# A fused decoder on one core: paired matmuls, GpSimd's share of the projections, and ScalarE's exponentials that write their own sums

## What is computed

```python
x = _layernorm(x + _L0_attn_ref(x, ...))         # self-attention, 16 heads of 16, quaternion projections, q and k normed
x = _layernorm(x + _L0_xattn_ref(ctx, x, ...))   # two memory hops over 77 context rows
x = _layernorm(x + _L0_ffn_ref(x, ...))          # 8 experts, 256 -> 1024 -> 256, gelu
x = _layernorm(x + _L1_attn_ref(x, ...))         # causal exponential convolution, gelu, projection
x = _layernorm(x + _L1_xattn_ref(x, ctx, ctx, ...))  # cross-attention, 16 heads of 16, 77 keys
x = _layernorm(x + _L1_ffn_ref(x, ...))          # gated layer, 256 -> 768 -> 256, everything quantised
```

```python
attn = jnp.einsum('bhqd,bhkd->bhqk', q, k) / jnp.sqrt(jnp.float32(Dh))
attn = jax.nn.softmax(attn, axis=-1)
out = jnp.einsum('bhqk,bhkd->bhqd', attn, v)
...
def act_qdq(x):
    qmax = 2.0 ** (ACT_BITS - 1) - 1.0
    scale = jnp.maximum(jnp.max(jnp.abs(x)) / qmax, 1e-12)
    return jnp.clip(jnp.round(x / scale), -qmax - 1.0, qmax) * scale
```

## Time and profile before

| | |
|---|---|
| median of 3 runs | 869.48 us |
| the profiled execution | 869.56 us, its span 867.8 us |
| busy: TensorE, weight loads | 752.1 us (87%), 431.9 us (50%) |
| busy: VectorE | 522.2 us (60%) |
| busy: ScalarE | 552.0 us (64%) |
| busy: GpSimd | 191.5 us (22%) |
| mean granted TensorE clock | 0.958 |
| chain that ended last | TensorE 38%, ScalarE 30%, VectorE 21%, issue 7% |

### The profile page before, as it was taken

One profiled execution on the slowest core, in us unless ns is written; L12 is line 12 of the kernel. 1 busy time (PEld: TensorE's weight loads), 2 busy tenths in 40 slices (PEclk: granted clock), 3 DMA queues, 4 the chain that ended last, 5 costly groups with the idle time before them and its releaser, 6 DMA issues.

```text
span 867.8 us, 10805 instructions
## 1 busy us (share of the span) xinstructions
PE 752.1 (87%) x3849; PEld 431.9 (50%) x3849; DVE 522.2 (60%) x1088; ACT 552.0 (64%) x941; POOL 191.5 (22%) x214
## 2 busy tenths in 40 slices
PE   4986899999999988998799998679899979994397
PEld 2642111111111137977688886445656844441286
DVE  4899332322111129779524648869967567898886
ACT  3656999999999962324132152575777433598991
POOL 1778000000000003215003202385543200000013
PEclk9996999999999999999899999799999989998599
DMA  7210213131364410302055000002100000000002
GB/s 198 100 25 1 49 33 78 26 85 25 87 202 66 118 47 1 97 1 98 1 194 193 1 1 1 0 0 74 37 0 2 1 1 0 1 0 0 0 25 73
DMA packets 57373, 42.13 MB, mean 49 GB/s; under 512 B 36866, under 2 KB 54120, under 8 KB 57192
## 3 DMA queue, kind: packets, MB, share of 16 engines
q1 hardware_dynamic: 57176, 41.31, 17.2%
q10 hardware_dynamic: 144, 0.13, 0.1%
HBM read 28.59 MB, written 4.46 MB: 38 GB/s over the span
## 4 chain that ended last, share of the span: by engine, by line
PE 38%; ACT 30%; DVE 21%; issue 7%; DMA 1%; SPq 1%; POOL 1%; DVEq 0%; POOLq 0%; ACTq 0%
ACT arena L535 24%; PE banks L1786 5%; PE banks L1778 5%; PE banks L1579 5%; PE banks L1567 5%; PE banks L1679 3%; PE banks L1651 2%; DVE arena L894 2%; DVE arena L902 2%; DVE arena L1186 2%; PE banks L1476 2%; DVE arena L790 2%; ACT arena L712 1%; ACT arena L698 1%; PE banks L1599 1%
## 5 line engine op out<-in xcount | busy, mean ns | idle before, releaser
L535 ACT ACTIVATE arena<-banks 128x1024 f32<-128x1024 f32 x256 | 235.4, 1094 | 3.1 <-PE banks L1349 3.0
L1349 PE MATMUL banks<-arena 128*32 128x512 f32 x1024 | 138.1, 611 | 2.2 <-ACT arena L535 0.8
L855 DVE COPY arena<-banks 128x512 f32<-128x512 f32 x16 | 11.1, 692 | 180.6 <-PE banks L1349 180.6
L1335 PE MATMUL banks<-arena 64*128 64x512 f16 x512 | 99.4, 390 | 23.1 <-ACT arena L535 9.4
L359 POOL TENSOR_SCALAR arena<-arena 128x2 f32<-128x2 f32 (+1 forms) x38 | 12.7, 334 | 462.2 <-DVE arena L897 462.2
L1335 PEld LDWEIGHTS banks<-arena 64*128 64x128 f16 x512 | 24.7, 93 | 166.8 <-ACT arena L535 154.4
L1778 PE MATMUL banks<-arena 128*128 128x512 f32 x192 | 85.9, 609 | 3.9 <-DVE arena L1197 3.7
L626 ACT ACTIVATE arena<-banks,arena 128x77 f32<-128x77 f32 x256 | 58.9, 363 | 22.2 <-DVE arena L1110 22.1
L1786 PE MATMUL banks<-arena 128*128 128x256 f32 x192 | 44.5, 397 | 26.6 <-ACT arena L733 26.6
L1579 PE MATMUL banks<-arena 128*128 128x256 f32 x256 | 58.2, 389 | 5.8 <-DVEq L1032 5.8
L1778 PEld LDWEIGHTS banks<-arena 128*128 128x128 f32 x192 | 37.3, 196 | 51.8 <-issue 48.8
(11 more groups left out here) (215 smaller groups left out, 1314.5 us busy)
## 6 DMA issues: line engine op xcount, KB each, us to landing
arena<-in_L_ffn_w SPq DMA_DIRECT2D x16, 1024.0 KB, 7.5
w_kept<-arena SPq DMA_DIRECT2D x3, 768.0 KB, 3.6
arena<-w_kept SPq DMA_DIRECT2D x3, 768.0 KB, 4.4
arena<-in_x SPq DMA_DIRECT2D x4, 512.0 KB, 8.7
out_x<-arena SPq DMA_DIRECT2D x3, 512.0 KB, 2.9
arena<-in_L_ffn_b SPq DMA_DIRECT2D x1, 1024.0 KB, 9.1
arena<-in_L_ffn_w_gate SPq DMA_DIRECT2D x1, 768.0 KB, 7.2
arena<-in_L_ffn_w_up SPq DMA_DIRECT2D x1, 768.0 KB, 8.9
```

Of the source, the lines that this page charges most:

```text
L535: act.activation(PT[kt % 2][:, half], PS[:, 2 * (n % 3):2 * (n % 3) + 2, :], ACT.Exp, scale=DH ** -0.5 / QK_UP ** 2).then_inc(sem("exp_don ...
L1335: mm = pe.matmul(bank(2 * (n % 3) + h), KT[u % 2][64 * h:64 * h + 64, P * kt:P * kt + P], QT[u % 2][64 * h:64 * h + 64, 512 * half:512 * h ...
L1349: mm = pe.matmul(PS[32 * j:32 * j + 32, 6, :], VS[w][:, kt, h, :], PT[kt % 2][:, half, h, :], start=(kt == 0), stop=(kt == TB - 1))
```

## The change

Six edits; the memory of the inputs and outputs stays.

1. Cross-attention's sums: each exponential of `numer` writes the sum of its 77 columns itself (`accum_out`, into the place in mxs where VectorE's sums went), and `denom` keeps the reciprocal alone.
2. Scores: each of the two matmuls of `xa_scores` takes only its 64 rows (`rows`) of the queries and keys.
3. Values: the chunks of the 616 columns are cut anew (CHUNK, ROWS): two of 128 inside heads 0 to 3, a mixed one of 104 in the middle, two of 128 inside heads 4 to 7. `p_turn` takes them in the order PAIRED, and `xa_values` multiplies the first four on 64 output rows each (`cut`), alternately the lower and the upper half; the mixed one keeps all 128. The masks and the values' projections use the same cut.
4. Projections: GpSimd no longer adds v's bias, which VectorE's `stage` brings in by two multiply-adds in place of one scaling; `low_part(t - 3)` of tiles 0 to 12 moves from VectorE to GpSimd, as two subtractions.
5. Ahead of the gated layer: the largest magnitude of x is spread by TensorE (`x_top`: a transpose of the 128 numbers into one row, VectorE's maximum of that row, a matmul with a row of ones, a copy), and group 0's quantisation is cut into its two halves, with a semaphore each.
6. The last quantisation: the first `ui` is cut into 512 and 1536 columns, and one small scale stands ahead of the wait.

```diff
+H4 = HC // 2
+REST = H4 * LC - 2 * P
+CHUNK = (0, P, 2 * P, 2 * P + 2 * REST, 3 * P + 2 * REST)
+ROWS = (P, P, 2 * REST, P, P)
+PAIRED = (0, 3, 1, 4, 2)
...
+            def low_part(t):
+
+                pool.wait_ge(sem("qn"), t + 1)
+                pool.wait_ge(sem("qk_hi"), t + 1)
+                u0 = NP * (t // TB)
+                src = qn[t % 2].rearrange("p m c d -> p m (c d)").rearrange("p m (u w) -> p m u w", u=NP)
+                for m in range(2):
+                    hi, lo = (QKH[:, m, u0:u0 + NP, t % TB, part, :] for part in range(2))
+                    ins = pool.tensor_tensor(lo, src[:, m], hi, ALU.subtract)
+                ins.then_inc(sem("qk_lo"), 1)
+
             pool.wait_ge(sem("quat_b"), 1)
             for t in range(T):
-                pool.wait_ge(sem("v_evac"), t + 1)
-                v = VV[:, NP * (t // TB):NP * (t // TB) + NP, t % TB, :]
-                pool.tensor_tensor(v, v, bq4[:, 2].rearrange("p (u w) -> p u w", u=NP), ALU.add).then_inc(sem("v_biased"), 1)
...
+                if t >= 3:
+                    low_part(t - 3)
...
-            largest(0, 0)
...
                     ins = act.activation(Ex[n % 4][:, h, :], PS[:, 2 * (n % 2) + h // 4, LC * (h % 4):LC * (h % 4) + LC], ACT.Exp,
-                                         scale=-1.0, bias=mxs[:, 8 * (n % 4) + h:8 * (n % 4) + h + 1])
+                                         scale=-1.0, bias=mxs[:, 8 * (n % 4) + h:8 * (n % 4) + h + 1],
+                                         accum_out=mxs[:, 32 + 8 * (n % 4) + h:33 + 8 * (n % 4) + h])
...
-                act.activation(ui[:, c, :], UF[:, c, :], ACT.Abs, scale=sc[:, 26:27]).then_inc(sem("f_ui"), 1)
+                for part in UI_FIRST if c == 0 else (slice(0, T * P),):
+                    act.activation(ui[:, c, part], UF[:, c, part], ACT.Abs, scale=sc[:, 26:27]).then_inc(sem("f_ui"), 1)
...
-                if t < T - 3:
-                    dve.wait_ge(sem("qk_hi"), t + 1)
-                else:
-
-                    link(dve.tensor_copy(hi, src))
+                link(dve.tensor_copy(hi, src))
                 dve.tensor_tensor(lo, src, hi, ALU.subtract).then_inc(sem("qk_lo"), 1)
...
+                    dve.tensor_scalar(bq4[:, 2], bq4[:, 2], ec, None, ALU.mult)
...
-                dve.tensor_scalar(VS[w][:, :, :, 0:DH], VV[:, u].rearrange("p t (h d) -> p t h d", h=2), ec, None, ALU.mult).then_inc(sem("vs"), 1)
+                for h in range(2):
+                    bias = bq4[:, 2, 2 * DH * (u % NP) + DH * h:2 * DH * (u % NP) + DH * h + DH]
+                    ins = dve.scalar_tensor_tensor(VS[w][:, :, h, 0:DH], VV[:, u, :, DH * h:DH * h + DH], ec,
+                                                   bias[:, None, :].to_broadcast([P, TB, DH]), ALU.mult, ALU.add)
+                ins.then_inc(sem("vs"), 1)
...
                 dve.wait_ge(sem("xa_e"), n + 1)
-                sums = mxs[:, 32 + 8 * (n % 4):40 + 8 * (n % 4)]
-                link(dve.tensor_reduce(sums, Ex[n % 4], AX.X, ALU.add))
-                dve.reciprocal(rdx[:, n % 4, :], sums).then_inc(sem("xa_rs"), 1)
+                dve.reciprocal(rdx[:, n % 4, :], mxs[:, 32 + 8 * (n % 4):40 + 8 * (n % 4)]).then_inc(sem("xa_rs"), 1)
...
-            dve.tensor_reduce(sc[:, 0:1], xmax, AX.X, ALU.max).then_inc(sem("amax"), 1)
-            dve.wait_ge(sem("gmax"), 1)
+            dve.tensor_reduce(sc[:, 0:1], xmax, AX.X, ALU.max).then_inc(sem("x_amax"), 1)
+            dve.memset(ones_row[0:1, :], 1.0)
+            dve.wait_ge(sem("x_amax_row"), 1)
+            dve.tensor_reduce(sc[0:1, 38:39], bank(2)[0:1, 0:P], AX.X, ALU.max).then_inc(sem("x_top"), 1)
+            dve.wait_ge(sem("x_top_all"), 1)
+            link(dve.tensor_copy(sc[:, 10:11], bank(3)[:, 0:1]))
 
             scale(10, 20, 1.0)
             for g in range(G4):
 
-                xt = XT[:, :, 512 * g:512 * g + 512]
                 dve.wait_ge(sem("xgT"), QFF_X + g + 1)
-                link(dve.tensor_scalar(xt, xt, sc[:, 22:23], MAGIC, ALU.mult, ALU.add))
-                dve.tensor_scalar(xt, xt, MAGIC, None, ALU.subtract).then_inc(sem("xq"), 1)
+                for k in ((slice(0, 1), slice(1, 2)) if g == 0 else (slice(0, KD),)):
+                    xt = XT[:, k, 512 * g:512 * g + 512]
+                    link(dve.tensor_scalar(xt, xt, sc[:, 22:23], MAGIC, ALU.mult, ALU.add))
+                    dve.tensor_scalar(xt, xt, MAGIC, None, ALU.subtract).then_inc(sem("xq"), 1)
...
-                dve.wait_ge(sem("f_ui"), c + 1)
-                ins = dve.tensor_tensor_reduce(spent, gi[:, c, :], ui[:, c, :], 1.0, 0.0, ALU.mult, ALU.max, accum_out=xmax[:, 8 + c:9 + c])
...
+                for n, part in enumerate(UI_FIRST if c == 0 else (slice(0, T * P),)):
+                    q = c + 1 if c else n
+                    dve.wait_ge(sem("f_ui"), q + 1)
+                    ins = dve.tensor_tensor_reduce(spent[:, part], gi[:, c, part], ui[:, c, part], 1.0, 0.0, ALU.mult, ALU.max, accum_out=xmax[:, 8 + q:9 + q])
...
                 for q in range(2):
-                    mm = pe.matmul(PS[:, 2 * (n % 2) + q, 0:4 * LC], qTx[g % 2][:, k, P * j:P * j + P],
-                                   Kbd[:, k, g // 2, 4 * q:4 * q + 4, :].rearrange("p h l -> p (h l)"), start=True, stop=True)
+                    rows = slice(64 * q, 64 * q + 64)
+                    mm = pe.matmul(PS[:, 2 * (n % 2) + q, 0:4 * LC], qTx[g % 2][rows, k, P * j:P * j + P],
+                                   Kbd[rows, k, g // 2, 4 * q:4 * q + 4, :].rearrange("p h l -> p (h l)"), start=True, stop=True)
...
-                for c in range(NC5):
-                    rows = LASTR if c == NC5 - 1 else P
-                    mm = pe.transpose(PS[0:rows, 4 + c // 4, P * (c % 4):P * (c % 4) + P], e[:, P * c:P * c + rows], ident)
+                for c, i in enumerate(PAIRED):
+                    mm = pe.transpose(PS[0:ROWS[i], 4 + c // 4, P * (c % 4):P * (c % 4) + P], e[:, CHUNK[i]:CHUNK[i] + ROWS[i]], ident)
...
                 for c in tiles:
-                    rows = LASTR if c == NC5 - 1 else P
-                    mm = pe.matmul(bank(b0 + k)[:, cols], Vx[0:rows, g // 2, k, c, :], PTx[g % 2][0:rows, NC5 * k + c, cols], start=(c == 0), stop=(c == NC5 - 1))
+                    i = PAIRED[c]
+                    if c < 4:
+                        cut = slice(64 * (c % 2), 64 * (c % 2) + 64)
+                        pe.matmul(PS[cut, b0 + k, cols], Vx[:, g // 2, k, i, cut], PTx[g % 2][:, NC5 * k + c, cols], start=(c < 2), stop=False)
+                    else:
+                        mm = pe.matmul(bank(b0 + k)[:, cols], Vx[0:2 * REST, g // 2, k, i], PTx[g % 2][0:2 * REST, NC5 * k + c, cols],
+                                       start=False, stop=True)
...
+            def x_top():
+
+                pe.wait_ge(sem("x_amax"), 1)
+                pe.transpose(bank(2)[0:1, 0:P], sc[:, 0:1], ident).then_inc(sem("x_amax_row"), 1)
+                pe.wait_ge(sem("x_top"), 1)
+                pe.matmul(bank(3)[:, 0:1], ones_row[0:1, :], sc[0:1, 38:39], start=True, stop=True).then_inc(sem("x_top_all"), 1)
+
             for g in range(G4):
+                if g == X_TOP_AT:
+                    x_top()
                 x_group_turn("ln_e", g + 1, QFF_X + g, g, b0=4)
...
-                    pe.wait_ge(sem("xq"), g + 1)
+                    pe.wait_ge(sem("xq"), g + 2 if g else 1)
...
                 for k in range(KD):
+                    if n == 0 and k:
+                        pe.wait_ge(sem("xq"), 2)
                     mm = pe.matmul(bank(2 + n % 4), (wgT if n < IC * G4 else wuT)[:, k, P * c:P * c + P], XT[:, k, 512 * g:512 * g + 512],
                                    start=(k == 0), stop=(k == KD - 1))
```

60 lines of the change are left out of this document (32 added, 28 removed).

## The result

| | before | changed |
|---|---|---|
| median of 5 runs | 869.48 us (868.73 to 872.59) | 863.87 us (862.72 to 865.12) |
| profiled execution, its span | 869.56, 867.8 us | 863.19, 861.5 us |
| busy: TensorE, weight loads | 752.1, 431.9 us | 741.3, 409.5 us |
| busy: VectorE | 522.2 us | 491.7 us |
| busy: ScalarE | 552.0 us | 575.0 us |

The account below looks back on a forecast made before the run. No engine bounds the whole span, so each edit was priced in its stage: cross-attention -8.2, projections -4, ahead of the gated layer -6.0, last quantisation +0.2, sum -18.0: from 869.48 to 851.5 us, range 839 to 870.

Parts of the forecast that it names:

- The read's price: Cross-attention, ScalarE: each accumulator read adds 0.09 us, 0.7 us a step, 23 us over 256 exponentials.
- A: Rival in cross-attention: a read costs about 0.04 us or less, half hidden; 843 us in all; chance 0.22.
- B: Rival in cross-attention: a read costs its whole 0.19 us; 869 us in all, no change; chance 0.11.
- C: Rival in cross-attention: accumulator read out before the next exponential, 0.25 us a read; 881 us in all; chance 0.11.
- edit 5 with both its parts: Ahead of the gated layer: -3.2 us without the clock's part, -2.8 from TensorE keeping full clock; together -6.0.
- rival E: Ahead of the gated layer: the clock falls all the same; 854.3 us; chance 0.44 together with the forecast.
- Edit 1's arithmetic: Cross-attention stretches where VectorE was full, sums moved to ScalarE's reads: 584 to 602 us -2, 602 to 628 us -1.
- Rival D: Projections: GpSimd becomes the bound, 3.94 us a tile, +8 in place of -4; 863.5 us; chance 0.12.
- by stretch, new busy time of each engine, the largest taken with 1 to 1.5 us of waits: Cross-attention: how each stretch's new length was priced; with the last values, -8.2 us in sum.
- the scores' pairing: Cross-attention, TensorE: two 64-row matmuls run side by side, a step's scores going from 1.04 to 0.52 us.
- the projections: Projections of the first attention: tiles 3.0 us apart in place of 3.32, over 13 tiles, -4 us.
- a slack of one tile: Projections: the next tile's sums of squares, queued behind GpSimd's new wait, could be one tile late.

Follow-up runs that it names:

- changed_again: The changed kernel run once more, unchanged, beside the other kernels: 862.7 us, ratio 0.9921 to the kernel before.
- before_with_reads: The kernel before, with only the cross-attention sums changed: each exponential writes its own sum, none on VectorE. 868.0 us, ratio 0.9962 to before.
- o_copies_first: The changed kernel, with ScalarE's copy of a finished group's values moved ahead of the exponentials of step n + 3: 857.9 us, ratio 0.9847 to before.
- copies_first_sums_split: The changed kernel, with ScalarE's copy of finished values ahead of the exponentials and, from step 20 on, sums on VectorE again: 854.0 us, ratio 0.9799.
- scores_30_repeated: The changed kernel, with the two scores matmuls of step 30 alone issued four times over: 861.6 us, ratio 0.9891 to the kernel before.
- sums_on_vectore: The changed kernel, with the cross-attention sums back on VectorE and all other edits kept: 859.0 us, ratio 0.9872 to the kernel before.
- sums_and_128_rows: The changed kernel, with sums back on VectorE and scores on all 128 rows again: 860.1 us, ratio 0.9881 to the kernel before.
- scores_128_rows: The changed kernel, with the scores matmuls on all 128 rows again: 860.6 us, ratio 0.9885 to the kernel before.

## Why the prediction was wrong, and where right

**Right.** The read's price (0.09 forecast and measured, rivals A, B and C out); who takes over in cross-attention (ScalarE); edit 5 with both its parts (-5.5 of -6.0), so rival E is out too; edit 6 (+0.2: from the last gate product to the last matmuls it is 27.15 us in the three profiles with the old quantisation and 27.34 to 27.36 in the other fourteen). Edit 1's arithmetic holds for the kernel that it was made on: 3 us forecast for VectorE's stretches, 3.3 measured alone. Rival D's 863.5 fits the measured time by accident: it needs tiles of 3.94, and they took 3.16.

**Wrong, the main step: "by stretch, new busy time of each engine, the largest taken with 1 to 1.5 us of waits".** It takes the largest sum of busy time for the length of a stretch. Where the time went, in starts of steps behind step 0 (read from ScalarE's timelines):

| | step 8 | 12 | 14 | 15 | 18 | 20 | 30 | 31 | row maximum |
|---|---|---|---|---|---|---|---|---|---|
| before | 35.7 | 54.7 | 62.5 | 67.1 | 77.9 | 84.2 | 123.6 | 126.9 | 148.2 |
| changed | 35.1 | 53.7 | 62.5 | 67.1 | 76.6 | 82.7 | 120.4 | 127.0 | 146.3 |
| changed_again | 34.9 | 54.3 | 63.1 | 69.3 | 78.4 | 84.4 | 122.3 | 128.6 | 147.9 |
| before_with_reads | 36.3 | 53.8 | 62.6 | 67.3 | 76.7 | 82.9 | 122.7 | 126.1 | 147.5 |
| o_copies_first | 35.5 | 54.3 | 61.7 | 66.4 | 75.9 | 82.5 | 118.5 | 121.5 | 140.5 |
| copies_first_sums_split | 34.9 | 54.4 | 61.9 | 66.5 | 76.1 | 82.6 | 116.4 | 118.7 | 137.9 |

Up to step 18 the forecast had -3 and the changed kernel -1.3 (+0.4 in changed_again). Behind it -3.5 were forecast to the last exponentials, and +1.4 came: 48.9 us from step 18 to 31 became 50.4. The end gave about what was forecast, 21.4 us from step 31 to the row maximum becoming 19.3 (-2.1 against -1.7). The 4.9 us missed from step 18 to 31 have two layers. The wait: eight exponentials with their reads stand ahead of the copy on ScalarE, and the paired TensorE, which is done with its values sooner, has nothing to cover it. With the copy moved those steps take 45.6, -3.3 against the -3.5 forecast. The clock: behind 2.1 us of that idle time the output product and what follows run at the 1.2 GHz level, which scores_30_repeated takes away. No run explains why only 1.3 of the 3 us came ahead of step 18. The forecast used just this on the gate's first products and didn't ask for it where its own lighter TensorE would wait. It named what is queued behind GpSimd's new wait, but not what is queued behind ScalarE's longer exponentials. A slip beside it changes nothing: for 584 to 602 its rows give ScalarE 13.7 and not 14.5, under the 16 taken.

**Wrong, a size: the scores' pairing.** Forecast 0.52 for two matmuls on 64 rows each; the chain has 0.72 (1.04 before). The values came closer: 1.86 from start to start for four half-high matmuls (two side by side twice, 1.72 at 0.43 a pass).
```profile
641.04 0.72 PE banks L1678 x4
```
**Wrong, a size: the projections,** 3.16 a tile and not 3.0, -1.7 us and not -4. Rival D's collisions are real: a pair of subtractions takes 1.30 alone (0.65 each, not 0.73) and 1.75 with one collision, in turn, so that every second tile has one. GpSimd is nearly full, idle 0.41 us in two tiles.
```profile
49.53 1.75 POOL L380 TENSOR_TENSOR arena<-arena 128x256 f16<-128x256 f32 x2
53.34 1.30 POOL L380 TENSOR_TENSOR arena<-arena 128x256 f16<-128x256 f32 x2
```
The forecast gave the sums behind GpSimd's new wait "a slack of one tile" and didn't price another wait: the norm of a tile writes into one of two buffers and waits for the low part of two tiles earlier, which is now behind GpSimd's sums. VectorE in the kernel after:
```profile
51.39 0.95 DVE L810 RECIPROCAL arena<-arena 128x128 f32<-128x128 f32 x1 [0.44 <-POOL arena L380]
54.74 0.95 DVE L810 RECIPROCAL arena<-arena 128x128 f32<-128x128 f32 x1 [0.85 <-POOL arena L380]
```
Whether this wait paces the tiles or GpSimd's own work does isn't shown; a third buffer wasn't tried. The rule of the Trainium skill (SBUF — State Buffer, "Who interferes with whom") that the forecast set beside D held in kind: VectorE's operations with two SBUF inputs and GpSimd's did lengthen each other (GpSimd's pair 1.75 against 1.30; VectorE's subtraction 1.22 against 0.69). What the forecast drew from it, 3.3 a tile and no gain, didn't come: 3.16 and 1.7 us.

**Open.** Why two 64-row matmuls of 308 columns take 0.72 together; why the clock falls behind a wait for the copy in some executions and not in others. The length of the wait alone doesn't tell: behind 1.38 us the output product takes 3.55 in sums_on_vectore, behind 1.39 it takes 1.99 in sums_and_128_rows. Open too is what part of scores_128_rows' 3 us is the clock and what the shifted order of events. The runs of one kernel spread by 2 to 7 us, so medians alone don't settle terms under 1.5.

## What to carry to other kernels

When an engine's instructions get longer, list what stands behind them in its queue and who waits for that, even if the engine has room on the sum of busy times; a copy that frees another engine belongs ahead of long work once its input is ready by then. When TensorE's work gets lighter, look for the places where it now waits (2.12 us here) and ask what the work behind would take at half clock. An edit's worth depends on its company: accumulated sums gained 3.3 us alone and lost some 4.5 beside the other edits; with the copy moved they still lost 3.0 in steps 20 to 31, and whether they gain ahead of those wasn't tried by itself.

## What the runs showed of the hardware

- An accumulator read behind a 77-column exponential costs 0.09 us from start to start (0.30 against 0.21), though its row shows 0.20 or more of busy time (mean 282 ns); the busy column counts both overlapping rows and so overstates it (80.9 + 66.0 us for 256 pairs that start 0.30 apart, 77 us).
- More TensorE work can make a stretch shorter: 12 repeated passes in an idle stretch took the following output product from 3.78 to 1.99 us, and step 30 to 31 from 6.54 to 3.76.
- The clock was at its 1.2 GHz level behind waits of 2.12 us (output product 3.78) and of 1.38 (3.55), and at the full level behind another of 1.39 (1.99).
- Two float32 matmuls on 64 rows each, 308 columns: 0.72 us for both, 1.04 on full rows; eight passes of 512 columns on 64 output rows: 1.86 from start to the next group's start, against 3.44 for eight on 128 in the kernel before.
- VectorE's subtraction of 256 columns takes 0.68 while GpSimd works on SBUF, as long as one of 512 when GpSimd is still (0.69). No run shows the 256 columns beside a still GpSimd.
